# The high halves of two products of a recurrent step made on GpSimd instead of VectorE

## What is computed

```python
def step(H, xs):
    xz, xr, xh = xs
    Z = jax.nn.sigmoid(xz + H @ Whz.T + bhz)
    R = jax.nn.sigmoid(xr + H @ Whr.T + bhr)
    H_tilda = jnp.tanh(xh + R * H @ Whh.T + bhh)
    H_new = Z * H + (1.0 - Z) * H_tilda
    Y = H_new @ Whq.T + bhq
    return (H_new, Y)
```

## Time and profile before

| | us |
|---|---|
| median of 3 runs | 283.1 (281.69 to 283.38) |
| the profiled execution | 281.84 |
| its span, first to last instruction | 279.8 |
| mean granted TensorE clock | 0.768 of full speed |
| DVE busy | 230.8 |
| GpSimd busy | 15.1 |

### The profile page before, as it was taken

The page is one execution under the profiler, slowest core; times in us unless marked ns, Lnnn a source line. Parts: engine busy times, 40 slices in busy tenths (PEclk is TensorE's granted clock), DMA queues, the critical chain, the costliest instruction groups (busy, mean ns, idle before and its releaser), DMA issues.

```text
span 279.8 us, 8339 instructions
## 1 busy us (share of the span) xinstructions
PE 241.6 (86%) x2834; PEld 171.6 (61%) x2834; DVE 230.8 (82%) x1552; ACT 130.6 (47%) x695; POOL 15.1 (5%) x19
## 2 busy tenths in 40 slices
PE   6987865889988998889988998899988998798896
PEld 6964644566655665566665665566665655466675
DVE  5874899888988988798979898898879888878873
ACT  1165555365434653465436643464436543344432
POOL 2692000000000000000000000000000000000000
PEclk9999555555898569955997579955996589859959
DMA  6930000000000000000000000000000000000000
GB/s 153 355 154 4 1 2 1 2 1 4 2 1 22 0 4 2 19 5 2 0 4 19 2 5 0 22 2 0 4 20 2 4 0 2 22 1 4 0 21 19
DMA packets 3369, 6.20 MB, mean 22 GB/s; under 512 B 757, under 2 KB 2093, under 8 KB 3200
## 3 DMA queue, kind: packets, MB, share of 16 engines
q1 hardware_dynamic: 2480, 3.86, 4.3%
q10 hardware_dynamic: 768, 1.72, 1.9%
q0 software_dynamic: 80, 0.11, 0.1%
HBM read 4.63 MB, written 1.05 MB: 20 GB/s over the span
## 4 chain that ended last, share of the span: by engine, by line
PE 50%; DVE 25%; ACT 10%; issue 7%; POOL 5%; DMA 3%; POOLq 0%
PE ZH L919 8%; PE R L919 6%; PE R L918 6%; PE ZH L918 6%; DVE m_p L738 6%; DVE rh_p L706 5%; ACT R L393 5%; ACT ZH L418 4%; PE O L804 3%; DMA const_sb<-consts 3%; PE F L859 3%; DVE rh_p L711 2%; PE F L786 2%; DVE zh_p L715 2%; DVE hid_lo L470 2%
## 5 line engine op out<-in xcount | busy, mean ns | idle before, releaser
L393 ACT ACTIVATE R<-R 128x16 f32<-128x16 f32 x128 | 21.5, 168 | 68.1 <-PE R L919 68.1
L418 ACT ACTIVATE ZH<-ZH 128x16 f32<-128x16 f32 x128 | 21.5, 168 | 57.2 <-PE ZH L919 56.7
L919 PE MATMUL R<-m_p,gru_hi 128*128 128x16 f16 x256 | 45.9, 180 | 0.0
L919 PE MATMUL ZH<-rh_p,gru_hi 128*128 128x16 f16 x256 | 42.9, 181 | 1.3
L919 PE MATMUL ZH<-m_p,gru_hi 128*128 128x16 f16 x256 | 38.0, 172 | 0.0
L918 PEld LDWEIGHTS ZH<-rh_p,gru_lo 128*128 128x128 f16 x128 | 13.1, 102 | 39.0 <-DVE rh_p L706 35.1
L918 PE MATMUL ZH<-rh_p,gru_lo 128*128 128x16 f16 x128 | 23.3, 182 | 13.8 <-DVE rh_p L706 5.8
L919 PEld LDWEIGHTS ZH<-rh_p,gru_hi 128*128 128x128 f16 x256 | 25.9, 105 | 12.3 <-DVE rh_p L711 0.2
L738 DVE TENSOR_TENSOR m_p<-keep,ZH 128x16 f16<-128x16 f32 x128 | 21.7, 169 | 14.2 <-ACT ZH L418 13.0
L706 DVE TENSOR_TENSOR rh_p<-R,hist 128x16 f16<-128x16 f32 x128 | 22.3, 174 | 11.9 <-ACT R L393 5.5
L918 PE MATMUL R<-m_p,gru_lo 128*128 128x16 f16 x128 | 23.6, 185 | 7.6 <-DVE m_p L738 1.3
(11 more groups left out here) (243 smaller groups left out, 767.2 us busy)
## 6 DMA issues: line engine op xcount, KB each, us to landing
x_sb<-xT SPq DMA_DIRECT2D x4, 256.0 KB, 8.0
xs_sb<-xsT SPq DMA_DIRECT2D x1, 1024.0 KB, 11.5
outT<-res SPq DMA_DIRECT2D x7, 128.0 KB, 1.9
ffn_sb<-ffn ACTq DMA_DIRECT2D x1, 512.0 KB, 6.3
w_sb<-w ACTq DMA_DIRECT2D x1, 512.0 KB, 11.0
w_sb<-w SPq DMA_DIRECT2D x1, 512.0 KB, 10.5
gru_sb<-gru ACTq DMA_DIRECT2D x1, 448.0 KB, 9.4
expand_sb<-expand ACTq DMA_DIRECT2D x1, 128.0 KB, 9.8
```

The source lines that it names most:

```text
L393: nc.scalar.activation(r_io, r_io, ACT.Sigmoid).then_inc(r_made, 1)
L418: nc.scalar.activation(c_io, c_io, ACT.Tanh).then_inc(cand_made, 1)
L919: return mm(out, gru_hi[:, WHR + gate, :], part, start=False, stop=low, skip_group_check=True)
```

## The change

GpSimd gets a loop over all 128 steps with two multiplications in each. The first waits for r and for the previous h and makes the high part of r times h; the second waits for the candidate and makes the high part of keep times candidate. Since r and the candidate are to be read by GpSimd, ACT now writes them to two new SBUF tiles of two buffers each, `r_sb` and `c_sb`, instead of in place in PSUM. DVE drops its two instructions for the high parts, reads r and the candidate from the new tiles, and waits for `rh_hi` and `m_hi` ahead of its two subtractions. PE's program is the same.

```diff
+        r_sb = sb("r_sb", [128, 2, B])
+        c_sb = sb("c_sb", [128, 2, B])
...
+            for k in range(K):
+                par = k % 2
+                for t in range(STEPS):
+                    p, q = t % 2, (t + 1) % 2
+                    step = k * STEPS + t
+                    pool.wait_ge(r_made, step + 1)
+                    pool.wait_ge(h_made, step + 1)
+                    nc.gpsimd.tensor_tensor(rh_p[:, p, 0, :], r_sb[:, p, :], hist_col(par, t - 1),
+                                            ALU.mult).then_inc(rh_hi, 1)
+                    pool.wait_ge(cand_made, step + 1)
+                    nc.gpsimd.tensor_tensor(m_p[:, q, 0, :], keep[:, p, :], c_sb[:, p, :],
+                                            ALU.mult).then_inc(m_hi, 1)
...
         @block.scalar
-                    r_io = R_bank[par][:, t * B:(t + 1) * B]
-                    nc.scalar.activation(r_io, r_io, ACT.Sigmoid).then_inc(r_made, 1)
+                    nc.scalar.activation(r_sb[:, p, :], R_bank[par][:, t * B:(t + 1) * B], ACT.Sigmoid).then_inc(r_made, 1)
...
-                    c_io = ZH_bank[par][:, N + t * B:N + (t + 1) * B]
-                    nc.scalar.activation(c_io, c_io, ACT.Tanh).then_inc(cand_made, 1)
+                    nc.scalar.activation(c_sb[:, p, :], ZH_bank[par][:, N + t * B:N + (t + 1) * B], ACT.Tanh).then_inc(cand_made, 1)
...
         @block.vector
-                    r_now = R_bank[par][:, t * B:(t + 1) * B]
-                    cand = ZH_bank[par][:, N + t * B:N + (t + 1) * B]
+                    r_now, cand = r_sb[:, p, :], c_sb[:, p, :]
                     dve.wait_ge(r_made, step + 1)
                     dve.wait_ge(h_made, step + 1)
-                    nc.vector.tensor_tensor(rh_p[:, p, 0, :], r_now, h_old, ALU.mult).then_inc(rh_hi, 1)
                     nc.vector.tensor_tensor(rh[:, p, :], r_now, h_old, ALU.mult).then_inc(rh_full, 1)
                     dve.wait_ge(z_made, step + 1)
                     nc.vector.tensor_tensor(zh_p[:, q, 0, :], z_sb[:, p, :], h_old, ALU.mult).then_inc(zh_hi, 1)
+                    dve.wait_ge(rh_hi, step + 1)
                     dve.wait_ge(rh_full, step + 1)
...
                     dve.wait_ge(cand_made, step + 1)
-                    nc.vector.tensor_tensor(m_p[:, q, 0, :], keep[:, p, :], cand, ALU.mult).then_inc(m_hi, 1)
                     nc.vector.tensor_tensor(m[:, q, :], keep[:, p, :], cand, ALU.mult).then_inc(m_full, 1)
+                    dve.wait_ge(m_hi, step + 2)
                     dve.wait_ge(m_full, step + 1)
```

## The result

Median of 4 runs 291.77 us (291.26 to 292.77) against 282.97 us; the ratio is 1.033, 95% interval 1.030 to 1.036. The profiled execution took 291.26 us, 9.4 us more than the one of before. Forecast were 315 us and 295 to 345: the sign is right, the size lies outside the range.

A forecast was written before the change was run, and what follows sets the result against it. The prediction took the high halves, for which PE waits twice a step, as the bound. 180 gates by 0.16 us (28.8 us) plus 4.6 us at the other 76 made 33.4 us on 281.8, so 315 us, range 295 to 345.

The forecast's parts named there:

- The duration of GpSimd's instruction: GpSimd's 128x16 multiplication for a high half, taken as 0.21 us from a rough line through two longer instructions.
- The handoffs: Around GpSimd's multiplication: 0.09 us from ACT onto GpSimd, 0.03 more for DVE's reading, and 0.11 from GpSimd to PE.
- the 0.16 in the sum: From sigmoid's end to PE's weight load: each gate 0.16 us later, 0.13 from GpSimd's path and 0.03 from DVE's reading.
- The 0.08 us from DVE to PE: In the kernel before, the handoff from L706's end to PE's waiting weight load, part of the 0.28 us path.
- The high halves are thus the gate through which PE gets its next work: PE's waits for L706 (40.9 us) and L738 (16.1 us) were read as what holds PE, twice in a step.
- the 180 gates: Places, of 256, where the high half was taken to be on the path; 180 by 0.16 is 28.8 us.
- I cost this at nothing: The low half's subtraction (L711) could start earlier with DVE relieved; counted as no gain because GpSimd's result comes later.
- ACT's write: ACT's activations into SBUF instead of PSUM: 10 ns by 256, 2.6 us, not counted in the sum but left in the range.
- faster: Rival: GpSimd needs 0.10 us with short handoffs, gates 0.07 us shorter, low half 3 us earlier; 266 us, chance 0.07.
- whole exclusion: Rival: GpSimd starts only when DVE's multiplication ends, 0.23 us more per gate; 48.6 us more, 330 us, chance 0.30.
- L720's length: Sign of being wrong: DVE's L718 and L720 get longer while GpSimd reads, so exclusion works in the other direction too.
- The 12 us put on top of the range: PE's clock: longer waits might keep it at 1.2 GHz, costing 12 us in expert steps' matmuls; part of the upper end.

The follow-up runs named there:

- e_sbuf_out: Kernel before, with ACT writing r and the candidate to SBUF as in the change and both high halves still on DVE; ratio 1.0139, +3.9 us.
- e_extra_wait: Kernel before, with one more, already met wait (on DVE's own high half) ahead of the product's wait at each subtraction; 300.95 us, 1.063.
- the exchange: Changed kernel with high halves back on DVE and the float32 products on GpSimd instead; 289.82 us (1.023), again 289.87 us (1.024).
- e_swap: Kernel before, with DVE making the float32 product first and the high half second, in both places; ratio 1.0015.
- e_low_late: Kernel before, with unread scratch multiplications on DVE ahead of the subtractions, so only the low halves come later; 294.18 us, 1.039.
- e_no_overlap: Changed kernel, with DVE's float32 products held back until GpSimd has made the high half; 363.99 us in a single run.

## Why the prediction was right in sign and wrong in size

- **The duration of GpSimd's instruction** was right: 0.21 forecast, 0.223 measured.
- **The handoffs** were too dear: onto GpSimd 0.08 and not 0.12 us (0.09 and 0.03 for DVE's reading; nothing of the 0.03 is seen), from it to PE 0.05 and not 0.11. The length from the sigmoid's end to PE grew by 0.08 us, half of the 0.16 in the sum. With the write's 0.016 it is 0.10.
- **The 0.08 us from DVE to PE** isn't all a handoff. PE's weight load also waits for `keep`, and it starts 0.11 us after that activation's end in the kernel before, in `e_sbuf_out`, in `e_extra_wait` and in the exchange (medians), while behind the high half it starts 0.06 or 0.07 us. Where the high half comes clearly last (`e_swap`, the changed kernel) it starts 0.05 us behind it, from DVE and GpSimd alike. By this, part of what the list put down to L706 was a wait for `keep`; no run moved `keep` alone.
- **The step that failed** is the first of the prediction: "The high halves are thus the gate through which PE gets its next work", and with it the 180 gates, and the low half ("I cost this at nothing"). PE did wait in 189 places for the high half, but ahead of a product that isn't done before its low part, for which it would have waited anyway. `e_swap` delayed the high halves by 0.09 us and cost at most 1.2 us where the theory asked for 16; `e_extra_wait` and `e_low_late` delayed the low halves and cost 18 and 11 us. The wait before the low product hardly stands in the list of waits (PE waits for L711 once, 0.2 us, although its matmul started 0.06 us behind L711 in 116 steps), and the earlier trace rows put a few places only on L711. The likely reason, not tested, is that the ends of PE's matmuls are modelled and long. What shows it are that constant 0.06 and the equal length of most half steps, which I had before me and did not measure.
- **By the low half** the sum is short. Before: handoff 0.032, issue of the second product 0.092, its 0.164, handoff to the subtraction 0.034, together 0.322 us from ACT's end. After: 0.078 + 0.223 + 0.034 = 0.335. Plus ACT's 0.016: 0.029 us, 256 times, is 7.4 us. These are medians; by the mean start of the subtraction, 0.033 us later, it is 8.4. Measured are 8.8 in the ring. The forecast's own terms (0.09 onto GpSimd, 0.21, 0.01 for the write), put into this sum with the 0.04 of the earlier trace rows ahead of L711, would have given 8 us.
- **ACT's write**, put aside as 2.6 us in the range, is real and nearly half of the loss: 3.9 us measured (16 ns, where 10 were read from L396).
- **The two sides hide each other.** GpSimd makes the high half slower by itself, but runs beside DVE's product. The 0.09 us of issue that DVE no longer needs before it pays for most of the dearer instruction (0.059 us) and handoff (0.046). The forecast named this gain in its rival "faster" and took 3 us for it.
- **Contention.** The rival *whole exclusion* (GpSimd's instruction waits for the whole of DVE's) does not occur: GpSimd starts 0.04 us after DVE's product has started, not after its end, and takes 2 to 4 ns more than alone. The Trainium skill ("SBUF — State Buffer", section "Who interferes with whom") expects the second to issue to be held until the first is through; on these 16-column instructions only L720, which starts third of the three, is longer, by 32 ns. L720's length was one of the prediction's signs of being wrong, and it came, but off the path.
- **The clock** stayed: 0.775 against 0.768. The 12 us put on top of the range did not come. The period of a step, for which 2.2 us were forecast, has a median of 1.96 us, where it was 1.90.

Settled are the path, the share of the write and the place of the rest. Not settled are the last 0.4 us of the ring, why `e_sbuf_out` costs 2 us less than its subtraction's start says, and why the first sigmoid comes up to 1.4 us later in some of the kernels; so it isn't shown that this part of the 9.4 us belongs to the change.

## What to carry to other kernels

A wait in the list says that an engine stood still, not that the wait is on the path; where an instruction needs two inputs that come one behind the other, delay each by itself, or look for the one whose start keeps a constant distance to the next event of the ring. When nearly every step of a loop has the same length whatever else runs in it, that ring is the bound, and it should be summed link by link before anything is moved. Of two waits on one DVE instruction, write first the one that is met last.

## What the runs showed of the hardware that was not expected

- On DVE two waits ahead of one instruction cost nothing when the one written last is met already (1.003), and 0.06 to 0.07 us each time when the one written last is the open one (1.063). It was seen in three kernels: 283.8 against 301.0, 291.6 against 307.1, and 289.9 against 306.7 us. With one met wait ahead of the open one DVE starts 0.10 us after the event, with two 0.13, with none 0.03 (`e_no_overlap` and the kernel before).
- A 16-column activation takes 184 ns into SBUF and 168 ns in place in PSUM, and the difference is on the path (`e_sbuf_out`, +3.9 us).
- GpSimd's 128x16 float32 multiplication takes 0.22 us, starts 0.08 us after ACT's end, and is read by DVE 0.03 and by PE 0.05 us behind its end: as a whole only 0.08 us more than on DVE.
